# Five expert tiles worked inside the last batch's routing chain, with no barrier between the two parts of the program

## The reference

```python
# B=8 batches of L=512 tokens, D=256; 16 heads; E=8 experts, top 2, F=1024
x = x + tanh(g0) * xattn(layernorm(x), ctx)        # hard-selected keys, softmax, Wc
z = layernorm(x)
top_v, top_i = top_k(z @ gate_w, 2); wts = softmax(top_v)
for e in range(8):
    h = gelu(z @ w1[e] + b1[e])
    out += comb[:, e] * (h @ w2[e] + b2[e])
x = x + tanh(g1) * out
```

## Time and profile before

| what | us |
|---|---|
| median of 3 runs (967.41 to 969.47) | 969.3 |
| the profiled execution | 969.38 |
| its span, first to last instruction | 967.2 |
| PE busy in the span | 802.4 (83%) |
| DVE / ACT / POOL busy | 512.6 / 368.6 / 426.0 |
| mean granted clock of PE | 0.916 |

### The profile page before, as it was taken

The page is one execution under the profiler, slowest core; times in us unless marked ns, Lnnn a source line. Parts: engine busy times, 40 slices in busy tenths (PEclk is TensorE's granted clock), DMA queues, the critical chain, the costliest instruction groups (busy, mean ns, idle before and its releaser), DMA issues. The chain is left out here.

```text
span 967.2 us, 20291 instructions
## 1 busy us (share of the span) xinstructions
PE 802.4 (83%) x6326; PEld 549.5 (57%) x6327; DVE 512.6 (53%) x1534; ACT 368.6 (38%) x770; POOL 426.0 (44%) x472
## 2 busy tenths in 40 slices
PE   3675899899898989788630199999999999999985
PEld 1233244444343534343230189898899889988874
DVE  3475576766776666774215144455444544445442
ACT  1312253635454363567520143333333333333331
POOL 4676463756656535465364013333333333333322
PEclk9877899979997999899765599999999999999998
DMA  5643324343525242233434222223222332223300
GB/s 165 142 98 131 57 89 77 111 100 120 112 88 129 77 93 66 82 114 107 131 109 132 86 42 45 44 46 58 47 44 42 49 55 48 44 44 45 46 10 3
DMA packets 63794, 75.56 MB, mean 78 GB/s; under 512 B 6384, under 2 KB 57456, under 8 KB 63600
## 3 DMA queue, kind: packets, MB, share of 16 engines
q1 hardware_dynamic: 50432, 57.81, 23.3%
q0 software_dynamic: 13296, 16.92, 10.1%
HBM read 46.75 MB, written 28.61 MB: 78 GB/s over the span
## 5 line engine op out<-in xcount | busy, mean ns | idle before, releaser
L2416 PE MATMUL ps_h<-x_hi,w_split 128*128 128x256 bf16 (+1 forms) x1248 | 201.0, 265 | 5.1 <-issue 5.1
L2425 PE MATMUL ps_y<-w_split,hidden 128*128 x1136 | 189.8, 273 | 1.6 <-DVE h_lo L2386 1.2
L714 ACT ACTIVATE prob<-ps_a 128x512 f32<-128x512 f32 x192 | 112.9, 603 | 181.6 <-PE ps_a L1143 108.2
L2416 PE MATMUL ps_h<-x_lo,w_split 128*128 128x256 bf16 (+1 forms) x624 | 162.6, 264 | 0.0
L2328 ACT ACTIVATE hidden<-ps_h,bias 128x256 f32<-128x256 f32 (+1 forms) x312 | 124.8, 451 | 96.6 <-PE ps_h L2416 96.5
L865 DVE TENSOR_REDUCE row_max<-ps_d 128x2 f32<-128x384 f32 x237 | 127.7, 550 | 59.8 <-PE ps_d L1123 58.2
L2425 PE MATMUL ps_y<-w_split,h_lo 128*128 x568 | 154.8, 273 | 0.0
L2302 POOL DMA_INDIRECT out<-y,token_at x71 | 117.8, 1659 | 41.6 <-POOL token_at L2300 30.3
L2416 PEld LDWEIGHTS ps_h<-x_hi,w_split 128*128 x1248 | 120.9, 98 | 20.6 <-issue 6.3
L2425 PEld LDWEIGHTS ps_y<-w_split,hidden 128*128 128x128 bf16 x1136 | 111.0, 98 | 17.3 <-issue 2.6
L2298 POOL TENSOR_TENSOR token_f<-tails,ones_f 128x2 f32<-128x2 f32 (+1 forms) x39 | 7.2, 185 | 257.1 <-DVE y L2375 253.6
(11 more groups left out here) (216 smaller groups left out, 1073.3 us busy)
## 6 DMA issues: line engine op xcount, KB each, us to landing
w_stage<-w SPq DMA_DIRECT2D x32, 512.0 KB, 4.3
xg<-queue SPq DMA_DIRECT2D x32, 260.0 KB, 2.8
w_split<-q_split SPq DMA_DIRECT2D x24, 256.0 KB, 8.4
x_in<-x SPq DMA_DIRECT2D x8, 512.0 KB, 4.3
ctx_sb<-ctx_t SPq DMA_DIRECT2D x8, 512.0 KB, 3.7
x<-x SPq DMA_DIRECT2D x8, 512.0 KB, 4.2
q_split<-q_hl SPq DMA_DIRECT2D x16, 256.0 KB, 3.4
out<-x SPq DMA_DIRECT2D x8, 512.0 KB, 5.5
```

Source lines behind the costliest of these rows:

```text
L714: a.activation(prob[n % 2][:, j, :], ps_a[i % 2][:], ACT.Exp, scale=SCALE).then_inc(exp_ready, 1)
L2416: last = t_.matmul(ps_h[n][:, c, 0:rows_of(i)], k.w1_split[:, bass.ds(e, 1), part, kt, f].rearrange("p a f -> p (a f)"), xs[s][:, kt, 0:ro ...
L2425: last = t_.matmul(ps_y[s][:, t, :], hs[s][:, f, token], k.w2_split[:, bass.ds(e, 1), part, f, :].rearrange("p a d -> p (a d)"), start=(f ...
```

## The change

Once batch 5 is in the queues (`EARLY_BATCHES = 6`), a small table names five tiles that are full already (`early_tables`, DVE, pass 7 step 2). These five tiles (`N_EARLY`) are worked inside `flow`. The 40 groups of 12 matmuls that make up their two layers are called beats; 15 of them stand between the steps of pass 8, 25 on the steps of pass 9. ACT does its part of a beat one step later than PE, DVE two steps later. Layer 2 of the five uses one bank (`ps_o`), layer 1 three. The tables of the remaining 34 tiles are made in pass 9 in four pieces, and the padding is written in pass 9. `flow` and `experts` become one block, so the barrier is gone, while the jump of `in_general` stays. The biases are loaded per tile by SP (`bias`, `b2`) and no longer all at once. In pass 8 the weight pieces move from steps (0, 1, 13, 24) to (0, 18, 22, 26). Buffers are shared between the two parts. In the diff, the first method `early` is that of `TileLoads` (SP), the second that of `TileTensor` (PE), the third that of `TileVector` (DVE); `prepare`, `h_lo` and `finish` are those of before, with the biases read from their own buffers.

```diff
+N_EARLY = 5
+EARLY_BATCHES = 6
+N_BEATS = 2 * PAIRS * N_EARLY
...
+def early_beat(b):
+    if b < PAIRS:
+        return 0, 1, b
+    slot, r = divmod(b - PAIRS, 2 * PAIRS)
+    if r < PAIRS and slot + 1 < N_EARLY:
+        return slot + 1, 1, r
+    return slot, 2, r % PAIRS
...
-        W_AT = {-2: (4, 10, 18, 26), -1: (4, 10, 18, 26), 6: (4, 10, 18, 26), 7: (4, 10, 18, 26), 8: (0, 1, 13, 24)}
+        W_AT = {-2: (4, 10, 18, 26), -1: (4, 10, 18, 26), 6: (4, 10, 18, 26), 7: (4, 10, 18, 26), 8: (0, 18, 22, 26)}
+        EARLY_BEATS = (2, 6, 9, 13, 14, 15, 17, 19, 21, 22, 23, 25, 27, 29, 30)
+        ACT_LATE, DVE_LATE = 1, 2
+        DVE_EARLY_TABLE, SP_EARLY, PE_EARLY, ACT_EARLY, DVE_EARLY = 2, 12, 20, 21, 23
+        SP_TILE = ((B, 5), (B, 18), (B, 29), (B + 1, 6), (B + 1, 14))
+        POOL_TILE = ((B, 29), (B + 1, 7), (B + 1, 15), (B + 1, 23), (B + 1, 28))
+        DVE_PADS, DVE_PARTS, DVE_OWNERS, DVE_EXPERTS, DVE_ROWS, SP_PADS = 1, 2, 5, 8, 11, 8
...
+                if step == SP_EARLY and p == B - 1:
+                    sp.wait_ge(tables_ready, 1)
+                    sp.wait_ge(scattered, 16 * 2 * LT * EARLY_BATCHES)
+                    tiles.early_begin()
+                if (p, step) in SP_TILE:
+                    tiles.early(SP_TILE.index((p, step)))
...
+def early_tables(v, chain, k, scratch, ready):
...
+    chain.then(v.tensor_scalar(k.rest_n[:], k.n_queued[:], 1.0 - P, None, ALU.add))
...
+    v.tensor_scalar(k.rest_n[:], k.taken[:], -float(TILE), None, ALU.mult).then_inc(ready, 1)
...
+    def early(self, i):
+        if i + 2 < N_EARLY:
+            self.rows(i + 2, i % 2)
+        if i + 1 < N_EARLY:
+            self.bias(i + 1, 1 - i % 2)
+        self.b2(i, i % 2)
...
+    def early(self, b):
+        i, layer, n = early_beat(b)
+        pe, t = self.pe, self.t
+        if layer == 1:
+            if n == 0:
+                if i + 1 < N_EARLY:
+                    self.early_turn(i + 1)
+                self.e[0] = load_expert(pe, self.k, i)
+                pe.wait_ge(t.x_lo_ready, i + 1)
+            bank = (PAIRS * i + n) % 3
+            self.banks.h[bank].wait_read(pe)
+            self.layer1(i, i % 2, self.e[0], n, self.m.early_h[bank])
+        else:
+            if n == 0:
+                self.e[1] = load_expert(pe, self.k, i)
+                pe.wait_ge(t.h_lo_ready, PAIRS * (i + 1))
+                self.banks.y.wait_read(pe)
+                self.banks.y.reader = (t.y_biased, i + 1)
...
+    def early(self, b):
+        i, layer, n = early_beat(b)
+        if layer == 1:
+            if n == 0 and i + 1 < N_EARLY:
+                self.prepare(i + 1, (i + 1) // 2, 1 - i % 2)
+            self.h_lo(i, i % 2, n)
+        elif n == PAIRS - 1:
+            self.finish(i, i // 2, i % 2, self.m.ps_y[0])
...
-        block = own.enter_context(nc.Block())
```

More of the change, by code:

```diff
@@ L786, in _ @@
                     a.copy(hi, stage).then_inc(w_hi, 1)
+                if step == ACT_EARLY and p == B - 1:
+                    tiles.split_x(0, 0)
+                for b in beats(p, step, ACT_LATE):
+                    tiles.early(b)
         @block.vector
@@ L1266, in _ @@
                     rank(e)
+                if step == PE_EARLY and p == B - 1:
+                    tiles.early_turn(0)
+                for b in beats(p, step):
+                    tiles.early(b)
+            wait_banks_e()
 def general_select(nc, k, sem, sb, ps, block):
@@ L2319, in body @@
+            tiles = TileScalar(nc, act, k, t)
             def body(i, half, s, more, two_more):
                 if more:
-                    split_x(i + 1, 1 - s)
-                if not first(i, 2):
-                    act.wait_ge(y_summed, i - 1)
+                    tiles.split_x(i + 1, 1 - s)
                 for n in range(PAIRS):
-                    act.wait_ge(h_ready, PAIRS * i + n + 1)
-                    for c in range(2):
-                        f = 2 * n + c
-                        last = a.activation(hidden[s][:, f, 0:rows_of(i)], ps_h[n][:, c, 0:rows_of(i)], ACT.Gelu, bias=bias[s][:, f:f + 1])
-                    last.then_inc(gelu_done, 1)
@@ new lines, in make_tables, with early @@
+                dve.wait_ge(tables_made, 1)
+                tables = Tables(v, chain, k, *m.scratch)
+                tables.parts()
+                tables.owners()
+                tables.experts()
+                tables.rows(tables_made)
+                chain.restart()
+            def early():
+                again = TileVector(nc, dve, k, k.tiles_again, chain)
+                again.prepare(0, 0, 0)
+                for b in range(N_BEATS):
+                    again.early(b)
+                chain.restart()
@@ L2379, in body @@
+            in_general(dve, general[0].dve, general[1].dve, make_tables, early)
+            tiles = TileVector(nc, dve, k, t, chain)
             def body(i, half, s, more, two_more):
@@ new lines, in early @@
+            def early():
+                again = TileTensor(nc, pe, k, k.tiles_again, TileBanks(Bank(), [Bank() for _ in range(3)], Bank()))
+                again.early_turn(0)
+                for b in range(N_BEATS):
+                    again.early(b)
+            in_general(pe, general[0].pe, general[1].pe, None, early)
+            tiles = TileTensor(nc, pe, k, t)
+            def turn(i, half, s):
+                pe.wait_ge(t.x_lo_ready, i)
+                tiles.turn(i, half, s)
+            def layer1(i, s, e, n):
+                pe.wait_ge(t.gelu_done, PAIRS * i if begins(i, N_EARLY + 1) else PAIRS * (i - 1) + n + 1)
+                tiles.layer1(i, s, e, n, m.ps_h[n])
@@ L2456, in body @@
+                if not begins(i, N_EARLY + 1) and not small:
                     whole_layer2(i - 1, 1 - s)
-            turn(0, 0, 0)
+            turn(N_EARLY, N_EARLY // 2, N_EARLY % 2)
             over_tiles(pe, body)
```

639 lines of the change are left out of this document (423 added, 216 removed).

## The result

The changed kernel takes 922.85 us (median of 4 runs, 920.69 to 924.47) against 968.46 us (4 runs, 967.41 to 969.47): ratio 0.9528, 95% interval 0.9503 to 0.9552. The forecast was 927, with 913 to 941 as its range. The profiled execution took 924.47 us with a span of 922.6 us and a mean granted clock of 0.942 (before 967.2 and 0.916).

A forecast was written before the change was run, and what follows sets the result against it. PE bounds the steady tiles; before them it idles in a 57 us hole that five tiles, 54.6 us of PE work, could fill. Tile 7's layer 1 moves from 626.0 to 584, so 42 us leave 969.4: 927, range 913 to 941.

The forecast's parts named there:

- pass 7 term: End of pass 7: early table makes batch 6's heads 3.4 us late, partly absorbed; +2 us, bounds 0 and +5.
- R: Instant when PE ranks the last batch: 513.13 us before the change, forecast at 522.
- Tile 2's rows: Pass 8: SP's row load waits behind weight piece 30, rows arrive at 501.5, PE stands about 7 us; the deciding term.
- From there to R: Pass 8, rows' arrival to PE ranking the last batch: 501.5 to 522, with 3 us for the slow clock.
- Pass 9: 25 beats 32.8 us, one turn 0.4, PE's waits 2.5: the last beat ends 36 us after the last ranking.
- The cover: Slots, scatter and pads end 10 us before the last beat does; without that, some 4 us of open row load.
- E: Instant when PE ends the last of the 40 beats, forecast at 558 us.
- The seam: Last beat to tile 5's layer 1, with the jump kept: 7.4 us; tile 7's layer 1 26 us after that beat.
- The chain not held: Rival: tile 2's rows come before PE asks, or the pause spares the clock; 918 us, chance 0.21.
- the beats hide nothing: Rival: each of pass 8's 15 beats delays the chain by its own length; about 940 us, chance 0.21.
- stay low: Rival: PE runs all 40 beats at clock 0.50, 105 us together; 985 us, slower, chance 0.02.
- The table loads: ACT: Exp between Gelus adds two table loads, 2.6 us; the skill's rule would make it 5.3.

The follow-up runs named there:

- The table later: Changed kernel with the five tiles' table made on DVE at step 6 of pass 7, behind batch 6's heads, not step 2: 925.87 us.
- the third piece moved: Changed kernel with the table at step 6, tile 0's turn at step 24, and pass 7's third weight piece split at step 20, not 18: 922.27 us.
- The rows first: Changed kernel with SP's load of tile 2's rows at step 2 of pass 8, ahead of weight piece 30's load, not step 5 behind it: 914.57 us.
- three tiles: Changed kernel with three early tiles instead of five, the other two worked among the rest: 934.74 us.
- with the barrier: Changed kernel with a meeting of all engines put back ahead of the flag and the jump: 943.13 us.

## Why the prediction was right

*What failed: the pass 7 term.* "I take +2 us at the end of pass 7" had the wrong sign. The table of five tiles does make the heads late by 3 us, as I reckoned (they run at 450.65 where the earlier trace rows has 447.30; S5 too is 0.35 later), but S5 to S6 is 2.2 us shorter, in all five rows with this pass 7, and S6 is at 481.08 where I had 484.95. I had read ACT's wait of 1.76 us for the piece as slack that gives part of the delay back. It was more: PE stood 2.65 us behind it and then ran at 0.50 for 10 us. With the late heads PE pauses for these instead, 2.27 us at 451, the clock stays 1.00 behind that, and ACT then comes late enough for the piece. The table later and the third piece moved show that what counts is where ACT waits for a late load, not the table. These 3.9 us are not the whole difference between 927 and 922.85, and other terms took part of them back: from the load of piece 30 to the turn are 5.1 us (4.4 foreseen), and the stretch to R is 1.05 longer. At R and at T7 some 2 us are left (519.87 for 522, 581.8 for 584). The rest lies behind T7 and in how far executions differ: the profiled one took 924.47, 1.6 above the median.

*Tile 2's rows.* Right as the deciding term: 7 us foreseen, 7.06 measured (6.8 to 8.0 in the other runs with this order), released by the row load behind the weight piece. The rows first price it at 9.1 us up to R, 8.3 in the time.

*From there to R.* 20.5 foreseen (501.5 to 522), 21.55 measured. The clock came back some 7 us after the turn. The sum was better than its terms: with the rows first and the clock at 1.00 the same stretch takes 19.65 us (491.48 to 511.13), 1.9 less. If that difference is the clock's, the 3 us that I put for it were too many and other terms too few.

*Pass 9.* R + 36 foreseen, 35.96 measured (519.87 to 555.83). For PE's waits on DVE, at the one bank of layer 2 and behind the tables, I allowed 2.5 us; they are 1.9, one of 0.32 for `h_lo` at 521.77 and two for the add of the tile before:

```profile
533.50 0.41 PE L470 MATMUL ps_o<-w_split,hidden 128*128 x2 [0.63 <-DVE prob L422]
...
550.40 0.41 PE L470 MATMUL ps_o<-w_split,hidden 128*128 x2 [0.99 <-DVE prob L422]
```

*The cover.* I put slots, scatter and pads some 10 us ahead of E; the tables end at 541.5 and the pads at 545.1 with E at 555.83. What ends last was named wrongly in my expectation of three tiles: there it is the tables.

*The seam.* E + 7.4 foreseen, 8.2 measured, just above the 7 to 8 that I had named as a sign: the jump took 3.43 us on DVE, where SP's of the earlier trace rows took 2.86. Without flag and jump the seam is 4.0. T7 is E + 26.0 (E + 26 foreseen), 44.1 us earlier than before (581.8 and 625.9); the spans differ by 44.6.

*The rivals.* The chain not held was a matter of one number in SP's order, which I had called fixed: with that number changed the time is 914.6. That the beats hide nothing is refuted by the same run (R is 29.66 us behind S6 there, 30.18 before). The clock was 1.00 from 506 to 556, so it didn't stay low; with the rows first it was full through all of pass 8, although the beats are scattered there. Between 440 and 840 us of the changed kernel it fell twice, in the pause of 7.06 us and in that of the seam.

*The table loads.* ACT in the changed kernel around R:

```profile
517.23 0.84 ACT L375 ACTIVATE hidden<-ps_a,narrow 128x256 f32<-128x256 f32 x2 [0.95 <-PE ps_a L460]
518.08 1.28 ACT L1148 ACT_TABLE_LOAD   x1
519.38 0.21 ACT L1148 ACTIVATE ratio<-gap 128x4 f32<-128x4 f32 x1
519.60 1.28 ACT L375 ACT_TABLE_LOAD   x1
520.90 0.84 ACT L375 ACTIVATE hidden<-ps_d,narrow 128x256 f32<-128x256 f32 x2
```

Each load begins 0.01 us behind the instruction before and the next begins 0.02 us behind it: 2.6 us for both switches. The Trainium skill, "ScalarE: Activation LUTs", section "What ACT_TABLE_LOAD costs", counts 2.66 us for one, a load and a drain. The trace agrees with the load (1.28 us) and shows no drain: 1.31 us lie between the two activations, and the measurement decides.

## What to carry to other kernels

When work is to fill the holes of a dependent chain, follow each of its loads through the queue that issues it: here one load behind another whose buffer came free late cost 9 us, and three steps further up it cost nothing. A barrier costs what its slowest engine still has to do and to drain (here 6 us behind POOL's last instruction), and the jump and the first load behind it; look at what must end before the next load can leave, and put work over that. A short wait on an engine that isn't the bound can cost more than its length: here ACT's wait of 1.66 us stood in a pass that was 2.9 us longer, with PE's clock low behind it, and a delay that did away with this wait was a gain.

## What the runs showed that I had not expected

- Pauses of PE of nearly one length had different ends: after 2.27 us in pass 7 of the changed kernel the clock stayed 1.00; after 2.65, 2.52 and 2.43 us in the kernel before and two of the experiments it was 0.50 for about 10 us; after 2.87 us, with the third piece moved, and after 2.05 us, in the same pass with the rows first, for about 3.5. The shortest of these pauses did not spare the clock, so the length of a pause alone doesn't tell.
- The drain of POOL lasted 9.05 us, 6 of them behind the end of its last instruction and 3 with nothing moving on the DMA engines.
- The gap behind the branch differed by engine and run: 2.50 us on SP with three tiles, 2.86 before, 4.13 with the barrier, 3.43 on DVE.
- S5 came between 445.6 and 448.0 us in kernels whose text is the same up to there: executions differ by 2 us before the change has any part in it.
